# Attention layers with written-out passes, a third bank of scores, and projections moved behind the scores

## The chip, the core and the metric

The kernel runs on one core of a Trainium2 chip. The core has five engines that run side by side: PE (TensorE, matrix products, with PEld for its weight loads), DVE (VectorE), ACT (ScalarE), POOL (GpSimd) and SP (SyncE, which starts DMAs). Each takes its own instructions strictly in order; semaphores make one wait for another. Products land in PSUM, eight banks of 128 partitions x 512 words of 32 bits; only DVE and ACT empty them here. The metric is the device time of one execution in microseconds (us).

## What is computed

Four transformer layers run one after the other on x, 16 sequences of 256 tokens with 128 features. Each adds an attention part and a feed-forward part to x, both fed with the layer-normed x:

```python
xn = _layernorm(x); x = x + attn_0(xn) + ffn_0(xn)   # sparse attention; experts with capacity
xn = _layernorm(x); x = x + attn_1(xn) + ffn_1(xn)   # 16 heads of 64, local mask; 8 experts, top 2
xn = _layernorm(x); x = x + attn_2(xn) + ffn_2(xn)   # 4 heads, windows; gated ternary network
xn = _layernorm(x); x = x + attn_3(xn) + ffn_3(xn)   # 16 heads of 64, causal; linear with a low-rank part
```

The second and the last layer share their attention:

```python
q, k, v = (x @ Wq, x @ Wk, x @ Wv) split into 16 heads of 64
attn = softmax(q @ k.T * 64 ** -0.5 + mask)
out = (attn @ v) joined @ Wo
```

In the second layer each token also passes experts: `relu(x @ up.T) ** 2 @ down.T`, weighted by a gate. In the last layer the linear feed-forward part is folded into the output projection.

## The kernel before

The function `attention` writes both 16-head layers. The work is 8 passes, and a pass has 2 sequences with 8 pairs of heads each, so 16 steps, s = 5 to 20; a `Fori` loop on every engine runs over the passes, and the 16 steps inside it are written out. The stages of one pair are spread over steps, so that step s handles the scores of pair s-2, the transposes of pair s-3 and the values of pair s-4 at once. Before the loop, a straight-line start fills this pipeline.

On PE a step is, in this order: scores of two heads (a mask through the identity matrix L1157, then the products L1160 and L1163 on two row halves of the array, written 64*128 in the trace), values (L1177, L1180, on two column halves, 128*64), six transposes (L1188, full array), in the second layer the experts' up projection (L1198 to L1200), the query and key projection of a later pair (`misc(i, s, "q")`, L1099 to L1101), in the second layer the down projection (L1210), and last what some steps have beside it: turns of the normed x ("t", L1091, s=6 and 14), value projections ("v", L1107 to L1109, s=8 to 11 and 16 to 19), gate logits ("g", L1144, second layer, s=8 and 16) and the output projection ("o", L1114 and L1119, s=12 and 20). Projections whose operands are split into a high and a low part take three matmuls per product.

DVE takes the maxima of the scores (L1358, L1359), copies the transposes out (L1365), inverts the sums (L1370), copies value projections out (L1391) and adds expert and output results to x (L1417, L1427). ACT does the exponentials (L1250, L1251, the sums coming with them), copies a pair's heads out (L1257), applies the experts' relu (L1262), copies queries and keys out (L1269) and turns out (L1236, L1237), in this order within a step. POOL multiplies by the inverted sums (L1472) and squares (L1485).

The order is that of the code; no scheduler changes it. What holds a bank back is a pair of counters per bank, full and empty. In the second layer query/key and value projections share bank 4, so a value projection waits until ACT's L1269 has emptied it. In the last layer values have bank 6. Scores of the two heads of a pair use banks 0 and 1; PE starts the next pair's scores when both heads' exponentials have been taken. Heads come out in bank 5, columns 0 to 255. "t", "g" and "o" use columns 256 to 511 of bank 5 in the second layer (there PE waits besides until the heads have been copied, L1128), and of bank 7 in the last.

Of the kernel before, what the change touches and what calls it, by code (L numbers as in the profile page):

```python
# [69 lines left out]
def program(nc, ins, out, upto=9):  # L70
# [3 lines left out]
    with ctx:  # L74
# [907 lines left out]
        def attention(name, layer, qk, mask, pack, phase, last_layer):  # L982
# [54 lines left out]

            BANK = {"q": 4, "v": 4, "t": 5, "g": 5, "o": 5} if moe else {"q": 4, "v": 6, "t": 7, "o": 7}
            side = PS[BANK["t"]][:, 256:512]
            shared = {}  # L1040
            for bk in sorted(set(BANK.values())):
                items = [m for m in MISC if BANK[m[1]] == bk]
                ahead = (BANK["t"] == bk) + sum(m[0] >= NP for m in items)
                key = {4: "q", 5: "t", 6: "v", 7: "t"}[bk]
                shared[bk] = (heir("at_full_" + key, len(items), ahead), heir("at_empty_" + key, len(items), ahead),
                              {m[1:]: k for k, m in enumerate(items)})
# [37 lines left out]
            def pe_(pe):  # L1084
# [38 lines left out]
                def misc(i, s, kinds):  # L1123
                    for at, kind, n in MISC:
                        if at != s or kind not in kinds:
                            continue
                        if moe and kind in "tgo":
                            pe.wait_ge(s_ot.s, s_ot.at(i, s - 4))  # L1128
# [21 lines left out]
                def step(i, s, least):  # L1150
                    j = s - 2
                    if j >= least:
                        pe.wait_ge(*read(i, "q", j))
                        pe.wait_ge(s_ex.s, s_ex.at(i, 2 * j - 1))
                        q = qp[j % 2]
                        for n in range(2):
                            pe.matmul(PS[n][:, m_from:384], ident16[:, :], mask[:, m_from:384], start=True, stop=False, skip_group_check=True)  # L1157
                        for n in range(2):
                            r = slice(64 * n, 64 * n + 64)
                            pe.matmul(PS[n][:, Q0], q[r, 0:128], q[r, 256:384], start=False, stop=True, skip_group_check=True)  # L1160
                        for n in range(2):
                            r = slice(64 * n, 64 * n + 64)
                            pe.matmul(PS[n][:, Q1], q[r, 128:256], q[r, 256:512], start=False, stop=True,  # L1163
                                      skip_group_check=True).then_inc(s_f.s, 1)
                    j = s - 4
                    if j >= least:
# [5 lines left out]
                        for at_, kind, n in MISC:  # L1172
                            if moe and kind in "tgo" and at_ == (s - 1 if s > FIRST else NP + FIRST - 1):
                                pe.wait_ge(*read(i, kind, n if s > FIRST else n - PER[kind]))
# [16 lines left out]
                    if moe and u >= least:  # L1191
# [9 lines left out]
                        mm.then_inc(f_u.s, 1)  # L1201
                    misc(i, s, "q")
                    u = s - 5
# [19 lines left out]
                pe.sem_inc(full_("o"), 1)  # L1223
                with pe.Fori(0, PASSES) as i:
                    for s in STEPS:
                        step(i, s, 0)

            def act_(act):
# [15 lines left out]
                def step(i, s, least):  # L1244
                    j = s - 2
                    if j >= least:
                        for g in (2 * j, 2 * j + 1):
                            act.wait_ge(s_mx.s, s_mx.at(i, g))
                            act.wait_ge(s_t.s, s_t.at(i, g - 4))
                            act.activation(pr[g % 4][:, Q0], PS[g % 2][:, Q0], ACT.Exp, bias=nmx[:, g % 4, 0:1], accum_out=sm[:, g % 4, 0:1])  # L1250
                            act.activation(pr[g % 4][:, Q1], PS[g % 2][:, Q1], ACT.Exp, bias=nmx[:, g % 4, 1:2],  # L1251
                                           accum_out=sm[:, g % 4, 1:2]).then_inc(s_ex.s, 1)
# [23 lines left out]
                for s in range(NP, NP + FIRST):  # L1276
                    step(-1, s, NP)
                with act.Fori(0, PASSES) as i:
                    for s in STEPS:
                        step(i, s, 0)  # L1280

            def dve_(dve):
# [6 lines left out]
                def settle(i):  # L1289

                    dve.wait_ge(dv.s, dv.before(k[0] - 1) if i is None or isinstance(i, int) else dv.at(i, k[0] - 1))

# [56 lines left out]
                def step(i, s, least):  # L1349
# [4 lines left out]
                    if j >= least:  # L1354
                        for g in (2 * j, 2 * j + 1):
                            dve.wait_ge(s_f.s, s_f.at(i, g))
                            dve.wait_ge(s_ex.s, s_ex.at(i, g - 4))
                            dve.tensor_reduce(nmx[:, g % 4, 0:1], PS[g % 2][:, Q0], AX, ALU.max, negate=True)  # L1358
                            dve.tensor_reduce(nmx[:, g % 4, 1:2], PS[g % 2][:, Q1], AX, ALU.max, negate=True).then_inc(s_mx.s, 1)  # L1359
                    for n in range(2):  # L1360
# [73 lines left out]
                dve.sem_inc(empty_("o"), 1)  # L1434
                with dve.Fori(0, PASSES) as i:
                    k[0] = 0
                    for s in STEPS:
                        step(i, s, 0)
                    assert k[0] == dv.n, (k[0], dv.n)

            def pool_(pool):
# [45 lines left out]
                for s in range(NP, NP + FIRST):  # L1487
                    step(-1, s, NP)
                with pool.Fori(0, PASSES) as i:
                    for s in STEPS:  # L1490
                        step(i, s, 0)
# [549 lines left out]
```

## Time and profile before

| | us |
|---|---|
| median of 3 runs | 2587.78 (2582.88 to 2591.21) |
| the profiled execution | 2596.73 |
| its span, first to last instruction | 2594.9 |
| second layer's steps, about | 694 to 1542 of the span |
| third layer, about | 1542 to 1997 |
| last layer's steps, about | 1997 to 2584 |
| PE busy, share of the span | 2255.4 (87%) |
| DVE, ACT, POOL busy | 1571.1, 1121.9, 1009.6 |
| mean granted clock of TensorE | 0.936 |

A busy time counts an engine's instructions; for PE the ends are modelled and successive matmuls overlap, so the distance from one start to the next tells more than a duration. "Idle before" gives how long an engine stood still ahead of an instruction and which engine's instruction released it; "issue" means that nothing in the profile explains it. The granted clock is 1.00 at 2.4 GHz and 0.50 at 1.2 GHz.

### The profile page before, as it was taken

The page shows a single profiled execution, that of the slowest core. Times are in us where ns is not written, and L with a number is a line of the kernel's source. Part 1 is how long each engine was busy: PE and PEld are TensorE (multiplying, and loading weights), DVE is VectorE, ACT ScalarE, POOL GpSimd, SP SyncE. Part 2 cuts the span into 40 slices and gives each one's busy share as a digit, 9 for nine tenths or more (in the row PEclk, how much of TensorE's full clock was granted, in tenths as well). Part 3 has the DMA queues.
Part 4 walks back from the last instruction along what each step waited for, and adds up shares of the span by engine and source line. Part 5 has one row for each costly group of instructions (what it writes and reads, how often), then busy time and mean ns, then how long its engine had stood idle before and what let it go on. Part 6 is the DMA issues. An engine that isn't in the chain of part 4 may idle for free.

```text
span 2594.9 us, 52767 instructions
## 1 busy us (share of the span) xinstructions
PE 2255.4 (87%) x15426; PEld 1689.0 (65%) x15426; DVE 1571.1 (61%) x4620; ACT 1121.9 (43%) x3580; POOL 1009.6 (39%) x1467
## 2 busy tenths in 40 slices
PE   2688888645599999999999989999997999999998
PEld 2466666423477777777777766666665777777676
DVE  3678877622465556565656556554555676666666
ACT  1233233011344444444544445554554555555554
POOL 2434444056444444444444451111113454444444
PEclk9989898568799999999999999999998999999999
DMA  4100000213300000000000000000000000000001
GB/s 159 35 1 0 0 0 0 71 37 27 108 2 2 2 2 2 1 2 2 2 2 1 2 1 1 0 0 0 0 0 1 2 0 1 1 1 1 1 1 33
DMA packets 31900, 32.56 MB, mean 13 GB/s; under 512 B 5472, under 2 KB 30048, under 8 KB 30816
## 3 DMA queue, kind: packets, MB, share of 16 engines
q1 hardware_dynamic: 26080, 25.99, 3.0%
q0 software_dynamic: 5632, 4.33, 1.3%
q8 instruction: 85, 1.39, 0.2%
q14 instruction: 103, 0.84, 0.1%
HBM read 21.79 MB, written 8.52 MB: 12 GB/s over the span
## 4 chain that ended last, share of the span: by engine, by line
PE 60%; issue 5%; ACT 5%; DVE 5%; POOL 1%; DMA 1%; DVEq 0%; ACTq 0%; SPq 0%; POOLq 0%
PE bank L1188 6%; PE bank L1177 5%; PE bank L1114 4%; PE bank L1163 4%; PE bank L1160 4%; PE bank L1210 4%; PE bank L1157 3%; PE bank L1099 2%; PE bank L1101 2%; PE bank L1100 2%; PE bank L1577 2%; PE bank L1599 2%; PE bank L1180 2%; PE bank L1601 2%; PE bank L1600 2%
## 5 line engine op out<-in xcount | busy, mean ns | idle before, releaser
L1472 POOL TENSOR_TENSOR work<-work 128x128 f32<-128x128 f32 (+1 forms) x1048 | 503.4, 512 | 795.6 <-DVE work L1370 795.6
L1250 ACT ACTIVATE work<-bank,work 128x128 f32<-128x128 f32 x524 | 191.8, 366 | 673.7 <-DVE work L1359 673.7
L1365 DVE COPY work<-bank 128x384 f32<-128x384 f32 x520 | 282.9, 548 | 42.2 <-PE bank L1188 16.3
L1251 ACT ACTIVATE work<-bank,work 128x256 f32<-128x256 f32 x524 | 247.4, 472 | 0.0
L1358 DVE TENSOR_REDUCE work<-bank 128x1 f32<-128x128 f32 x524 | 149.6, 285 | 151.5 <-PE bank L1163 129.2
L1188 PE MATMUL bank<-w_const,work 128*128 128x128 f32 x1560 | 230.8, 285 | 0.0
L1359 DVE TENSOR_REDUCE work<-bank 128x1 f32<-128x256 f32 x524 | 216.6, 413 | 0.0
L1188 PEld LDWEIGHTS bank<-w_const,work 128*128 128x128 f32 x1560 | 168.4, 142 | 46.6 <-issue 46.6
L1391 DVE COPY work<-bank 128x512 f32<-128x512 f32 x136 | 94.0, 691 | 164.4 <-PE bank L1109 155.5
L1177 PE MATMUL bank<-work 128*64 128x256 f32 x1032 | 174.0, 416 | 0.1
L1269 ACT ACTIVATE work<-bank 128x512 f32<-128x512 f32 x266 | 162.3, 610 | 11.8 <-PE bank L1101 10.7
L1099 PE MATMUL bank<-l_xn_hi,l_qk_hi 128*128 128x256 f32 x532 | 164.2, 309 | 2.8 <-DVE l_xn_lo L1314 2.7
L1163 PE MATMUL bank<-work 64*128 64x256 f32 x1048 | 166.2, 395 | 0.0
L1157 PE MATMUL bank<-mask,ident 128*128 128x384 bf16 (+1 forms) x524 | 121.0, 314 | 36.1 <-ACT work L1251 20.7
L1100 PE MATMUL bank<-l_xn_lo,l_qk_hi 128*128 128x256 f32 x532 | 151.6, 285 | 0.0
L1101 PE MATMUL bank<-l_xn_hi,l_qk_lo 128*128 128x256 f32 x532 | 151.1, 284 | 0.0
L1210 PE MATMUL bank<-w_l,work 128*128 128x128 f32 x1024 | 134.9, 275 | 0.0
L1160 PE MATMUL bank<-work 64*128 64x128 f32 x1048 | 134.7, 335 | 0.0
L1485 POOL TENSOR_TENSOR work<-work 128x512 f32<-128x512 f32 x129 | 134.1, 1040 | 0.0
L1160 PEld LDWEIGHTS bank<-work 64*128 64x128 f32 x1048 | 82.7, 193 | 73.5 <-issue 73.5
L1210 PEld LDWEIGHTS bank<-w_l,work 128*128 128x128 f32 x1024 | 125.0, 191 | 0.0
L1417 DVE SCALAR_TENSOR_TENSOR x_sb<-bank,work,x_sb 128x128 f32 x256 | 77.5, 344 | 66.0 <-PE bank L1210 65.6
(330 smaller groups left out, 5414.0 us busy)
## 6 DMA issues: line engine op xcount, KB each, us to landing
w_l<-in_l SPq DMA_DIRECT2D x1, 3210.5 KB, 10.4
w_l<-in_l SPq DMA_DIRECT2D x1, 3080.0 KB, 22.2
w_f<-in_f SPq DMA_DIRECT2D x1, 3072.0 KB, 15.2
x_sb<-in_x SPq DMA_DIRECT2D x4, 512.0 KB, 5.8
normed_rows<-work SPq DMA_DIRECT2D x1, 2048.0 KB, 9.6
residual<-x_sb SPq DMA_DIRECT2D x1, 2048.0 KB, 9.4
qk<-in_qk SPq DMA_DIRECT2D x2, 1024.0 KB, 7.8
x_sb<-residual SPq DMA_DIRECT2D x4, 512.0 KB, 6.0
```

Of the source, the lines that this page charges most:

```text
L1099: pe.matmul(to, qk_hi[:, n, ws], x, start=True, stop=False)
L1100: pe.matmul(to, qk_hi[:, n, ws], xr, start=False, stop=False)
L1101: mm = pe.matmul(to, qk_lo[:, n, ws], x, start=False, stop=True)
L1160: pe.matmul(PS[n][:, Q0], q[r, 0:128], q[r, 256:384], start=False, stop=True, skip_group_check=True)
L1163: pe.matmul(PS[n][:, Q1], q[r, 128:256], q[r, 256:512], start=False, stop=True, skip_group_check=True).then_inc(s_f.s, 1)
L1177: pe.matmul(PS[5][r, 0:256], v[:, 0, h], pt[(2 * j + n) % 4][:, 0:256], start=True, stop=False, skip_group_check=True)
L1188: mm = pe.transpose(PS[2 + g % 2][:, to * 128:(to + 1) * 128], pr[g % 4][:, c * 128:(c + 1) * 128], ident)
L1210: mm = pe.matmul(PS[7][:, t * 128:(t + 1) * 128], h2[u % 2][:, c * 256 + t * 128:c * 256 + (t + 1) * 128], L["down"][:, (2 * e + c) * D:(2 ...
L1251: act.activation(pr[g % 4][:, Q1], PS[g % 2][:, Q1], ACT.Exp, bias=nmx[:, g % 4, 1:2], accum_out=sm[:, g % 4, 1:2]).then_inc(s_ex.s, 1)
L1359: dve.tensor_reduce(nmx[:, g % 4, 1:2], PS[g % 2][:, Q1], AX, ALU.max, negate=True).then_inc(s_mx.s, 1)
L1365: dve.tensor_copy(pt[g % 4], PS[2 + g % 2][:, 0:384]).then_inc(s_te.s, 1)
L1472: ins = pool.tensor_tensor(w, w, spread(rc[:, g % 4, q:q + 1], w.shape[1]), ALU.mult)
```

## The change

Three edits. The four `Fori` loops over the passes become Python loops, so the 8 passes are written out as straight code and every wait compares with a constant. In the last layer three banks (0, 1 and 7) take the scores of heads in turn, and PE's wait for exponentials is one head looser there; the turns and the output projection move from bank 7 to bank 5, with the second layer's waits. In both layers `misc(i, s, "q")` moves from behind the transposes (second layer: from behind the up projection) to right behind the scores. The core of the diff:

```diff
-            BANK = {"q": 4, "v": 4, "t": 5, "g": 5, "o": 5} if moe else {"q": 4, "v": 6, "t": 7, "o": 7}
+            BANK = {"q": 4, "v": 4, "t": 5, "g": 5, "o": 5} if moe else {"q": 4, "v": 6, "t": 5, "o": 5}
+            SCORE = (0, 1) if moe else (0, 1, 7)
+
+            def scored(i, g):
+
+                return PS[SCORE[(i * NH + g) % len(SCORE)]]
...
-                        if moe and kind in "tgo":
+                        if kind in "tgo":
                             pe.wait_ge(s_ot.s, s_ot.at(i, s - 4))
...
-                        pe.wait_ge(s_ex.s, s_ex.at(i, 2 * j - 1))
+                        pe.wait_ge(s_ex.s, s_ex.at(i, 2 * j + 1 - len(SCORE)))
...
-                            pe.matmul(PS[n][:, Q1], q[r, 128:256], q[r, 256:512], start=False, stop=True,
+                            pe.matmul(scored(i, 2 * j + n)[:, Q1], q[r, 128:256], q[r, 256:512], start=False, stop=True,
                                       skip_group_check=True).then_inc(s_f.s, 1)
+                    misc(i, s, "q")
                     j = s - 4
...
-                            if moe and kind in "tgo" and at_ == (s - 1 if s > FIRST else NP + FIRST - 1):
+                            if kind in "tgo" and at_ == (s - 1 if s > FIRST else NP + FIRST - 1):
                                 pe.wait_ge(*read(i, kind, n if s > FIRST else n - PER[kind]))
...
-                    misc(i, s, "q")
                     u = s - 5
...
-                with pe.Fori(0, PASSES) as i:
+                for i in range(PASSES):
                     for s in STEPS:
                         step(i, s, 0)
```

The other engines' uses of `PS[n]` and `PS[g % 2]` for scores become `scored(...)`, and their loops change as PE's does. A line of the kernel before stands 5 lines further down in the changed one up to the scores, and up to 6 further behind them.

Where the instructions stand, in three places. First PE in the second layer, step s=9: from the end of the up projection to the value projection. bank6 holds up, bank4 the projections, bank7 down; the names in brackets are the counters waited for, `at_empty_q` being bank 4's. Before:

```order
L1200 MATMUL bank6<-l1_xn_hi_0_49,l1_up_lo_58 128x256
L1133 REGISTER_ALU
L1099 MATMUL bank4<-l1_xn_hi_1_50,l1_qk_hi_53 128x256 [waits at_normed_split,at_empty_q]
L1100 MATMUL bank4<-l1_xn_lo_1_52,l1_qk_hi_53 128x256
L1101 MATMUL bank4<-l1_xn_hi_1_50,l1_qk_lo_55 128x256
L1099 MATMUL bank4<-l1_xn_hi_1_50,l1_qk_hi_53 128x256
L1100 MATMUL bank4<-l1_xn_lo_1_52,l1_qk_hi_53 128x256
L1101 MATMUL bank4<-l1_xn_hi_1_50,l1_qk_lo_55 128x256
L1210 MATMUL bank7<-w_l1,work 128x128 [waits moe_added,moe_square]
L1210 MATMUL bank7<-w_l1,work 128x128 x3
L1133 REGISTER_ALU
L1107 MATMUL bank4<-l1_wv_hi_54,l1_xn_hi_1_50 128x512 [waits at_normed_split,at_empty_q]
```

and now:

```order
L1205 MATMUL bank6<-l1_xn_lo_0_51,l1_up_hi_57 128x256
L1206 MATMUL bank6<-l1_xn_hi_0_49,l1_up_lo_58 128x256
L1215 MATMUL bank7<-w_l1,work 128x128 [waits moe_added,moe_square]
L1215 MATMUL bank7<-w_l1,work 128x128 x3
L1112 MATMUL bank4<-l1_wv_hi_54,l1_xn_hi_1_50 128x512 [waits at_normed_split,at_empty_q]
L1113 MATMUL bank4<-l1_wv_lo_56,l1_xn_hi_1_50 128x512
L1114 MATMUL bank4<-l1_wv_hi_54,l1_xn_lo_1_52 128x512
```

The six query/key matmuls are gone from between up and down, and the value projection's wait for bank 4 stands where it stood. Second, PE in the last layer, an early step, from the scores on: bank5 takes the values, bank2 the transposes. Before:

```order
L1163 MATMUL bank0<-work 128x256
L1163 MATMUL bank1<-work 128x256
L1167 REGISTER_ALU
L1168 REGISTER_ALU [waits at_turned_out]
L1177 MATMUL bank5<-work 64x256 [waits at_heads_out]
L1177 MATMUL bank5<-work 64x256
L1180 MATMUL bank5<-work 64x128 x2
L1185 REGISTER_ALU
L1186 REGISTER_ALU [waits at_weights]
L1188 MATMUL bank2<-w_const,work 128x128 [waits at_turned_out]
L1188 MATMUL bank2<-w_const,work 128x128 x2
```

and now:

```order
L1168 MATMUL bank7<-work 128x256
L1168 MATMUL bank0<-work 128x256
L1104 MATMUL bank4<-l3_xn_hi_0_67,l3_qk_hi_71 128x256 [waits at_normed_split,at_empty_q]
L1105 MATMUL bank4<-l3_xn_lo_0_69,l3_qk_hi_71 128x256
L1106 MATMUL bank4<-l3_xn_hi_0_67,l3_qk_lo_73 128x256
L1104 MATMUL bank4<-l3_xn_hi_0_67,l3_qk_hi_71 128x256
L1105 MATMUL bank4<-l3_xn_lo_0_69,l3_qk_hi_71 128x256
L1106 MATMUL bank4<-l3_xn_hi_0_67,l3_qk_lo_73 128x256
L1183 MATMUL bank5<-work 64x256 [waits at_heads_out,at_turned_out]
L1183 MATMUL bank5<-work 64x256
L1186 MATMUL bank5<-work 64x128 x2
```

The projections now stand between the row halves of the scores and the column halves of the values, the scores are in banks 7 and 0 here, and the register work of the loop is gone. Third, PE in the last layer at a turn (L1091, which is L1096 in the changed kernel). Before:

```order
L1100 MATMUL bank4<-l3_xn_lo_0_69,l3_qk_hi_71 128x256
L1101 MATMUL bank4<-l3_xn_hi_0_67,l3_qk_lo_73 128x256
L1130 REGISTER_ALU
L1133 ISA [waits at_normed]
L1091 MATMUL bank7<-w_const,work 128x128 [waits at_empty_t]
L1091 MATMUL bank7<-w_const,work 128x128
L1154 REGISTER_ALU [waits at_empty_q]
L1157 MATMUL bank0<-mask3,ident16 128x256 [waits at_exps]
L1157 MATMUL bank1<-mask3,ident16 128x256
```

and now:

```order
L1194 MATMUL bank2<-w_const,work 128x128 [waits at_turned_out,at_weights]
L1194 MATMUL bank2<-w_const,work 128x128 x2
L1194 MATMUL bank3<-w_const,work 128x128 [waits at_turned_out,at_weights]
L1194 MATMUL bank3<-w_const,work 128x128 x2
L1096 MATMUL bank5<-w_const,work 128x128 [waits at_empty_t,at_normed,at_heads_out]
L1096 MATMUL bank5<-w_const,work 128x128
L1162 MATMUL bank1<-mask3,ident16 128x256 [waits at_exps,at_empty_q]
L1162 MATMUL bank7<-mask3,ident16 128x256
```

The turn is in bank 5 with `at_heads_out`, ACT's copy of this step's heads, among its waits, and it follows the transposes directly.

## Rows read from the trace of the kernel before

**Rows 1.** Windows by stage: length, busy us of PE, PEld, DVE, ACT, POOL, clock, DMA

```profile
694.00:1542.00 848.00, 801.18 (x6456) 641.63 (x6452) 507.81 (x1660) 399.93 (x1467) 388.05 (x662) 0.97 0.01 2
...
1997.00:2584.00 587.00, 564.99 (x4652) 423.29 (x4650) 400.14 (x1241) 328.84 (x1322) 270.37 (x550) 0.98 0.00 1
```

**Rows 2.** Waits in the second layer: who waited for whom, us, times, longest

```profile
PE bank L1107 <- ACT work L1269: 33.2, 17, 2.3
...
PE bank L1157 <- issue: 12.8, 7, 2.0
```

**Rows 3.** Waits in the last layer: who waited for whom, us, times, longest

```profile
DVE work L1358 <- issue: 18.9, 7, 2.9
...
PE bank L1157 <- ACT work L1251: 19.4, 16, 2.7
```

**Rows 4.** Timeline, second layer, step s=11: start, us, engine, line, tiles, count [idle]

```profile
948.83 0.28 PE L1200 MATMUL bank<-l_xn_hi,l_up_lo 128*128 128x256 f32 x1
...
948.95 0.28 PE L1099 MATMUL bank<-l_xn_hi,l_qk_hi 128*128 128x256 f32 x1
...
949.34 0.62 ACT L1262 ACTIVATE work<-bank 128x512 f32<-128x512 f32 x1
...
949.66 1.05 PE L1210 MATMUL bank<-w_l,work 128*128 128x128 f32 x8
949.86 0.60 ACT L1269 ACTIVATE work<-bank 128x512 f32<-128x512 f32 x1
...
950.51 0.50 PE L1107 MATMUL bank<-l_wv_hi,l_xn_hi 128*128 128x512 f32 x1
```

**Rows 5.** Timeline of PE, last layer's straight-line start, projections right behind scores

```profile
1988.48 0.60 PE L1163 MATMUL bank<-work 64*128 64x256 f32 x4
1989.01 0.39 PE L1099 MATMUL bank<-l_xn_hi,l_qk_hi 128*128 128x256 f32 x1
...
1989.83 0.40 PE L1107 MATMUL bank<-l_wv_hi,l_xn_hi 128*128 128x512 f32 x1
```

**Rows 6.** Timeline of PE, third layer, from full array to 32-column tiles

```profile
1588.71 0.39 PE L1600 MATMUL bank<-lo_hA,hi_h 128*128 128x512 f32 x1
1588.94 0.39 PE L1601 MATMUL bank<-hi_hA,lo_h 128*128 128x512 f32 x1
1589.26 0.64 PE L1634 MATMUL bank<-work 128*32 128x256 f32 x8
```

**Rows 7.** Timeline, last layer, step s=13: PE, and what ACT does at its end

```profile
2179.67 0.38 PE L1157 MATMUL bank<-mask,ident 128*128 128x256 bf16 x2
...
2180.31 0.60 PE L1163 MATMUL bank<-work 64*128 64x256 f32 x4
...
2180.84 0.65 PE L1177 MATMUL bank<-work 128*64 128x256 f32 x4
...
2182.40 0.36 ACT L1250 ACTIVATE work<-bank,work 128x128 f32<-128x128 f32 x1
...
2183.19 0.39 ACT L1257 ACTIVATE work<-bank 128x256 f32<-128x256 f32 x1
...
2183.37 0.39 PE L1157 MATMUL bank<-mask,ident 128*128 128x256 bf16 x2
```

**Rows 8.** Timeline, second layer, step s=9: the value projection waits

```profile
937.21 0.50 PE L1107 MATMUL bank<-l_wv_hi,l_xn_hi 128*128 128x512 f32 x1 [2.08 <-ACT work L1269]
```

**Rows 9.** Windows, second layer, first 3.69 us of step s=10

```profile
938.01:941.70 3.69, 3.69 (x20) 1.88 (x20) 2.75 (x9) 0.79 (x4) 0.26 (x1) 0.54 0.00 0
```

**Rows 10.** Timeline of PE, last layer, step s=17, which has a value projection

```profile
2194.88 0.39 PE L1157 MATMUL bank<-mask,ident 128*128 128x256 bf16 x2
...
2198.29 0.40 PE L1107 MATMUL bank<-l_wv_hi,l_xn_hi 128*128 128x512 f32 x1
...
2198.98 0.39 PE L1157 MATMUL bank<-mask,ident 128*128 128x256 bf16 x2
```

**Rows 11.** The page: DMA queue, kind, packets, MB, share of the engines

```profile
q8 instruction: 85, 1.39, 0.2%
```

More of the change, by code:

```diff
@@ L1043, in attention @@
                 ahead = (BANK["t"] == bk) + sum(m[0] >= NP for m in items)
-                key = {4: "q", 5: "t", 6: "v", 7: "t"}[bk]
+                key = {4: "q", 5: "t", 6: "v"}[bk]
                 shared[bk] = (heir("at_full_" + key, len(items), ahead), heir("at_empty_" + key, len(items), ahead),
@@ L1153, in step @@
                         pe.wait_ge(*read(i, "q", j))
-                        pe.wait_ge(s_ex.s, s_ex.at(i, 2 * j - 1))
+                        pe.wait_ge(s_ex.s, s_ex.at(i, 2 * j + 1 - len(SCORE)))
                         q = qp[j % 2]
                         for n in range(2):
-                            pe.matmul(PS[n][:, m_from:384], ident16[:, :], mask[:, m_from:384], start=True, stop=False, skip_group_check=True)
+                            pe.matmul(scored(i, 2 * j + n)[:, m_from:384], ident16[:, :], mask[:, m_from:384], start=True, stop=False, skip_group_check=True)
                         for n in range(2):
                             r = slice(64 * n, 64 * n + 64)
-                            pe.matmul(PS[n][:, Q0], q[r, 0:128], q[r, 256:384], start=False, stop=True, skip_group_check=True)
+                            pe.matmul(scored(i, 2 * j + n)[:, Q0], q[r, 0:128], q[r, 256:384], start=False, stop=True, skip_group_check=True)
                         for n in range(2):
                             r = slice(64 * n, 64 * n + 64)
-                            pe.matmul(PS[n][:, Q1], q[r, 128:256], q[r, 256:512], start=False, stop=True,
+                            pe.matmul(scored(i, 2 * j + n)[:, Q1], q[r, 128:256], q[r, 256:512], start=False, stop=True,
                                       skip_group_check=True).then_inc(s_f.s, 1)
+                    misc(i, s, "q")
                     j = s - 4
@@ L1249, in step @@
                             act.wait_ge(s_t.s, s_t.at(i, g - 4))
-                            act.activation(pr[g % 4][:, Q0], PS[g % 2][:, Q0], ACT.Exp, bias=nmx[:, g % 4, 0:1], accum_out=sm[:, g % 4, 0:1])
-                            act.activation(pr[g % 4][:, Q1], PS[g % 2][:, Q1], ACT.Exp, bias=nmx[:, g % 4, 1:2],
+                            act.activation(pr[g % 4][:, Q0], scored(i, g)[:, Q0], ACT.Exp, bias=nmx[:, g % 4, 0:1], accum_out=sm[:, g % 4, 0:1])
+                            act.activation(pr[g % 4][:, Q1], scored(i, g)[:, Q1], ACT.Exp, bias=nmx[:, g % 4, 1:2],
                                            accum_out=sm[:, g % 4, 1:2]).then_inc(s_ex.s, 1)
@@ L1277, in act_ @@
                     step(-1, s, NP)
-                with act.Fori(0, PASSES) as i:
+                for i in range(PASSES):
                     for s in STEPS:
@@ L1289, in settle @@
                 def settle(i):
-                    dve.wait_ge(dv.s, dv.before(k[0] - 1) if i is None or isinstance(i, int) else dv.at(i, k[0] - 1))
+                    dve.wait_ge(dv.s, dv.before(k[0] - 1) if i is None or i < 0 else dv.at(i, k[0] - 1))
                 def stats(i, tile):
@@ L1357, in step @@
                             dve.wait_ge(s_ex.s, s_ex.at(i, g - 4))
-                            dve.tensor_reduce(nmx[:, g % 4, 0:1], PS[g % 2][:, Q0], AX, ALU.max, negate=True)
-                            dve.tensor_reduce(nmx[:, g % 4, 1:2], PS[g % 2][:, Q1], AX, ALU.max, negate=True).then_inc(s_mx.s, 1)
+                            dve.tensor_reduce(nmx[:, g % 4, 0:1], scored(i, g)[:, Q0], AX, ALU.max, negate=True)
+                            dve.tensor_reduce(nmx[:, g % 4, 1:2], scored(i, g)[:, Q1], AX, ALU.max, negate=True).then_inc(s_mx.s, 1)
                     for n in range(2):
@@ L1434, in dve_ @@
                 dve.sem_inc(empty_("o"), 1)
-                with dve.Fori(0, PASSES) as i:
+                for i in range(PASSES):
                     k[0] = 0
@@ L1488, in pool_ @@
                     step(-1, s, NP)
-                with pool.Fori(0, PASSES) as i:
+                for i in range(PASSES):
                     for s in STEPS:
```

## The prediction

> **What bounds the kernel now.** I read the windows by stage first. In the second layer PE is busy 801 of 848 us, in the last layer 565 of 587 us, while DVE, ACT and POOL stay at or under 69% of either stage [rows 1]. So these two stages run at PE's pace, and a change there is worth what it does to the stretch from one step's first L1157 to the next. The waits say what is left over. In the second layer PE sat idle 33.2 us in 17 waits before the value projection L1107, for ACT's copy L1269 out of bank 4, and 12.8 us in 7 waits before a scores group L1157 with nothing named ("issue"): seven is the number of times that an eight-pass loop jumps back [rows 2]. In the last layer DVE sat 18.9 us before L1358 on "issue", again 7 times, and PE then waited 19.4 us for the exponentials [rows 3]: there the loop's end is paid by DVE and handed on.
>
> **Term 1: the written-out loops.** They remove 14 loop ends, 7 in each layer (the eighth leaves the loop). The idle time that the view shows is 12.8 and 19.4 us. A matmul row of 0.28 us hides the next start by about 0.17 us, since those of one kind start 0.12 us apart [rows 4], so an idle interval is longer than shown by that: 7 times 0.17 makes 14 us in the second layer, 16 times 0.17 makes 22 us in the last. Gain 36 us. It could be less if DVE's and PE's new straight code ran into late instruction loads, at most all 36.
>
> **Term 2: the projections behind the scores.** No instruction is added, but a change of how PE's array is divided is. A step now goes: mask on the full array, scores on two row halves (64*128), values on two column halves (128*64), transposes, projections on the full array, which is three switches. After the change it goes full, rows, full, columns, full: four. The straight-line start of the last layer already holds the new sequence's first half: from L1163 to L1099 0.53 us, and from there to the next full matmul 0.82 us [rows 5]. In its old place the same six matmuls take 0.71 us (948.95 to 949.66) [rows 4]. The switch from full to columns stands in the third layer: L1601 is followed after 0.32 us by L1634, where two full ones stand 0.23 us apart, so 0.09 us [rows 6]. From L1163 to L1177 is 0.53 us today [rows 7]. New: 0.53 + 0.82 + 0.09 = 1.44 us; old: 0.53 + 0.71 = 1.24 us. So 0.20 us more in each step that PE bounds. L1634 has 32 columns and not 64, so the last 0.09 is by a neighbour; its bounds are 0 and the 0.11 that the row switch adds (0.82 less 0.71), and a step costs between 0.11 and 0.22 us. I take 0.20.
> The Trainium skill's page "TensorEngine Tiling (Array Packing)", under Key Properties, says that changing the tiling mode drains TensorE. It gives no price; by it the switch can't be free, and it speaks against this edit where PE is the bound. The rows above agree, with 0.09 to 0.11 us.
>
> **Term 3: in the second layer ACT's copy comes later.** ACT takes a step's work in a fixed order: exponentials, heads, relu L1262 of the up projection, then L1269, which empties bank 4. The value projection needs that bank and ends PE's step. In step s=11 all fits: relu at 949.34, L1269 from 949.86 to 950.46, L1107 at 950.51 without a wait [rows 4]. After the change the up projection stands behind the moved one. Its last L1200 starts at 948.83 + 0.71 + 0.20 = 949.74 and ends 0.28 us later, 950.02; relu at about 950.06, L1269 0.52 us after it at 950.58, over at 951.18, L1107 at 951.23. PE is there at 950.51 + 0.20 = 950.71. That is a wait of 0.52 us where there was none. It meets value steps s=8, 10, 11, 16, 18 and 19. In s=9 and 17 PE already waits 2.08 us, for an ACT that the gate work on DVE made late [rows 8]; up is long done there, so L1107 keeps its time and the 0.20 of term 2 disappears in the wait.
> Per pass: 8 steps without values at 0.20 = 1.6 us, six at 0.72 = 4.3 us, two at 0: 5.9 us, times 8 = 47 us. Less 14 from term 1: the second layer loses 33 us. The waits of 2 us are followed by a stretch of 3.69 us at a granted clock of 0.54, one level being 1.2 and the other 2.4 GHz [rows 9]; since these waits shrink by 0.2 us only, I leave both stretches of a pass in place.
>
> **Term 4: three banks of scores in the last layer.** A value step is bound by PE: 3.41 us up to L1107 and 4.10 us in all [rows 10]. A step without values takes 3.70 us, so it waits 0.29 us for the exponentials of the step before [rows 7]. With a third bank it need only wait for the first head of the pair. ACT is through with that one about when it starts the second (2182.40), and with both about when it turns to L1257 (2183.19) [rows 7]: 0.8 us earlier, so the wait goes. But the step then costs 3.41 + 0.20 = 3.61 us. Four such steps (s=5, 7, 13, 15) gain 0.09 each, 0.4 us; eight value steps lose 0.20 each, 1.6 us.
>
> **Term 5: what the third bank pushes out.** The turns (s=6, 14) and the output projection (s=12, 20) move from bank 7 to the second half of bank 5, and PE must first wait until ACT has copied this step's heads out (L1257). In s=13 that copy starts 3.52 us after the step's first L1157 and takes 0.39 us [rows 7]: the bank is free at 3.96, PE would be there at 3.61. A turn step today is 3.70 us too, its two turns hidden in the exponentials' wait; it becomes 3.96 + 0.22 = 4.18, so 0.48 more. An output step pays 0.20 + 0.35 = 0.55 more. Together 2.1 us a pass. If ACT is as late as it may be, 0.3 us more on each of the four; if early, 0.35 less: between 0.7 and 3.3 us. The reader's side (the next values wait for DVE's or ACT's reading) is covered by scores and projections, 1.44 us.
> Last layer per pass: -0.4 + 1.6 + 2.1 = 3.3 us, times 8 = 26 us, less 22 from term 1: 4 us slower.
>
> **Covers.** POOL's products start after DVE's copies of the transposes, which come 0.9 us later in a step; the next step's transposes are later by the same, so nothing is late. The scores wait for nothing new. The last layer's mean granted clock is 0.98 [rows 1], so at most 2% of 587 us, 12 us, are lost to half clock; without the waits of 2 us at its loop ends these stretches should go, but part of them lies in waits already counted in term 1. I take a third, -4 us (0 to -12).
>
> **The sum.** 33 + 4 - 4 = +33 us on the profiled execution, whose span is 2594.9 us and its time 2596.73. The median of the runs is 2587.78, 9 us lower; I let the difference carry over: 2621 us.
>
> **Rivals.**
> A, the switches are free (PE drains while it would wait anyway). The term of 0.20 goes everywhere, the waits of terms 3 and 5 stay: second layer 6 x 0.52 x 8 = 25, less 14; last layer (-0.29 x 4 + 2 x 0.48 + 2 x 0.55) x 8 = 7, less 22. With -4 for the clock: 11 - 15 - 4 = -8 us, 2580 us. Rows 5 and 6 speak against it.
> B, faster: neither switch nor wait costs, because straight code with constant waits lets ACT and PE run ahead. Then the loop ends (36) and the exponentials' waits (0.29 x 6 x 8 = 14) are gained, and 4 of the clock: 2534 us; with term 5 left in, 2551 us. For it speaks that the loop ends are real; against it that inside a step PE's starts are as close as in the straight-line start: L1163 to its follower is 0.53 us in both [rows 5, 7], so registers cost nothing there. It decides once a moved projection costs under 0.1 us a step and ACT's relu is not held up.
> C, the clock: the new waits of 0.5 us bring more half-clock stretches. Two more in each pass of the second layer cost 3.69 x 0.46 = 1.7 us each, 27 us: 2648 us. The other way, the two that are there could go: 2594 us.
> D, instruction loads. The straight code of both layers must be streamed. The page has 85 loads of 16 KB for one queue already [rows 11], as loops ask for their code in every pass, and the stretches of rows 4, 7 and 10 show no gap that a load would make; so I give a loss little. 
>
> **Chances.** Forecast 0.50 with its own range 2605 to 2640; A 0.13; B 0.12; C slower 0.10, C the other way 0.07; D 0.08. A change of 0.3% is 8 us. Faster by more than that: B and half of A, 0.18; within: the other half of A and a part of C's second way, 0.10; slower: the rest, 0.72. The range that leaves out most of B and the far end of C and D is 2568 to 2648.
>
> **What would show it.** In a profile of the changed kernel: no "issue" waits before the scores (term 1); scores to values 1.44 us with the projection between (2); a wait of about half a microsecond before the value projection in 6 more steps of each pass, ended by ACT's copy (3); no exponentials' wait in the last layer, steps of 3.6 and 4.3 us (4); the turns and the output projection waiting for the copy of the heads (5). The prediction is wrong if the second layer does not grow, or if a step without values there stays at its present length.

## The result: 1.1% slower

The changed kernel takes 2614.91 us (median of 4 runs, 2611.14 to 2617.06), the kernel before 2586.33 us (4 runs, 2582.88 to 2591.21). The ratio is 1.0108 with a 95% interval of 1.0087 to 1.0128, so it is 28.6 us slower; forecast were 2621 us and +33. In all that follows a ratio is to the kernel before on the same chip; 0.01 of it is 26 us. Lines behind the second layer's bank table stand 5 or 6 higher than before: L1157 is now L1162, L1163 L1168, L1099 L1104, L1177 L1183, L1107 L1112, L1200 L1206, L1262 L1267, L1269 L1274, and the copy of the heads L1257 is L1262.

The page of the profiled execution after (span; busy time of each engine; the first queue that loads instructions):

```profile
span 2615.3 us, 48911 instructions
...
PE 2298.1 (88%) x15410; PEld 1700.0 (65%) x15426; DVE 1521.8 (58%) x4620; ACT 1134.9 (43%) x3580; POOL 1012.5 (39%) x1467
...
q8 instruction: 103, 1.69, 0.3%
```

The span is 2615.3 us against 2594.9, and the loads of [rows 11] went from 85 to 103. A second queue that loads instructions went the other way, from 103 to 91, at half the bytes per load.

Windows over the eight passes of the second and of the last layer, from the first step's scores to the end of the last step; columns as in [rows 1]. First the kernel before, with its edges at these same points, then the kernel after:

```profile
696.20:1540.60 844.40, 798.44 (x6434) 639.24 (x6432) 504.73 (x1649) 397.74 (x1458) 386.54 (x660) 0.97 0.01 2
1999.20:2584.90 585.70, 563.68 (x4641) 422.35 (x4640) 398.29 (x1235) 327.02 (x1314) 269.75 (x549) 0.98 0.00 1
```

```profile
692.00:1556.30 864.30, 823.61 (x6434) 646.25 (x6432) 483.47 (x1651) 408.20 (x1458) 388.56 (x661) 0.98 0.01 1
...
2012.80:2605.50 592.70, 581.36 (x4642) 424.66 (x4639) 371.40 (x1237) 329.54 (x1317) 271.56 (x549) 1.00 0.01 2
```

The second layer grew from 844.4 to 864.3 us, +19.9, and the last from 585.7 to 592.7, +7.0. Together that is more than the difference of the spans (20.4): by the same edges, what lies ahead of the second layer came out 4.2 us shorter and the third layer 2.1. In the nine profiled executions of this document the second layer's first step of a pass (s=5) starts between 688.4 and 703.4 us, though the code ahead of it is the same, so 4.2 us there say nothing. PE's busy time rose by 25 us and 18 us, although the matmuls are the same (x6434; x4641 and x4642): most of the time that the moved projections cost in PE's order shows here as PE at work, not as a wait (how long a matmul lasts is modelled).

The waits after, in the second layer (who waited for whom: us in all, times, longest):

```profile
PE bank L1112 <- ACT work L1274: 40.7, 64, 1.7
```

Before, L1269 held L1107 for 33.2 us in 17 waits [rows 2]. Now the copy holds the value projection in 64 places, 8 in each pass, for 40.7 us. The row "issue" before the scores is gone in both layers, and so is PE's wait for the exponentials in the last [rows 2, 3]. What stands in the last layer instead:

```profile
PEld bank L1119 <- ACT work L1262: 7.4, 16, 0.5
PEld bank L1096 <- ACT work L1262: 6.9, 15, 0.5
...
PE bank L1104 <- DVE l_xn_lo L1319: 3.9, 15, 0.3
```

The first two are the output projection and the turns waiting for the copy of the heads. The third, for DVE's low part of the normed rows, was in no term.

Timeline after, second layer, s=11, which answers to [rows 4]:

```profile
943.41 0.50 PE L1162 MATMUL bank<-mask,ident 128*128 128x384 bf16 x2
...
944.17 0.60 PE L1168 MATMUL bank<-work 64*128 64x256 f32 x4
...
944.70 0.39 PE L1104 MATMUL bank<-l_xn_hi,l_qk_hi 128*128 128x256 f32 x1
...
945.61 0.65 PE L1183 MATMUL bank<-work 128*64 128x256 f32 x4
...
947.73 0.28 PE L1206 MATMUL bank<-l_xn_hi,l_up_lo 128*128 128x256 f32 x1
...
948.04 0.60 ACT L1267 ACTIVATE work<-bank 128x512 f32<-128x512 f32 x1 [0.59 <-PE bank L1206]
...
948.54 0.59 ACT L1274 ACTIVATE work<-bank 128x512 f32<-128x512 f32 x1
...
949.18 0.50 PE L1112 MATMUL bank<-l_wv_hi,l_xn_hi 128*128 128x512 f32 x1 [0.28 <-ACT work L1274]
...
949.99 0.50 PE L1162 MATMUL bank<-mask,ident 128*128 128x384 bf16 x2
```

From the scores L1168 to the values L1183 it is 945.61 - 944.17 = 1.44 us, with the projection L1104 between. The up projection's last L1206 starts at 947.73; behind it relu L1267, then the copy L1274 from 948.54 to 949.13, then L1112. The step is 6.58 us long (949.99 - 943.41), where the kernel before has 5.89: 0.69 more. Less the 0.20 that scores to values took, PE lost 0.49 us ahead of L1112. The trace calls only 0.28 us of it idle, since the matmul before hides the rest (as in term 1).

Timeline after, last layer, s=13, which answers to [rows 7]:

```profile
2198.10 0.38 PE L1162 MATMUL bank<-mask,ident 128*128 128x256 bf16 x2
...
2201.63 0.39 ACT L1262 ACTIVATE work<-bank 128x256 f32<-128x256 f32 x1
2201.69 0.27 PE L1162 MATMUL bank<-mask,ident 128*128 128x256 bf16 x1
```

The next scores start 3.59 us after the step's first ones, before the copy of the heads (2201.63) is done; before it was 3.70 us and, as the prediction reads [rows 7], they waited for the exponentials.

### The profile page after: what moved, and what is told of

Read it like the earlier page. It is cut to its first block, busy times and chain, and to the rows that moved or that the text cites. A ratio compares the mean times of both kernels' runs of the same rounds, so it can differ in the third digit from the quotient of the medians.

```text
span 2615.3 us, 48911 instructions
## 1 busy us (share of the span) xinstructions
PE 2298.1 (88%) x15410; PEld 1700.0 (65%) x15426; DVE 1521.8 (58%) x4620; ACT 1134.9 (43%) x3580; POOL 1012.5 (39%) x1467
## 3 DMA queue, kind: packets, MB, share of 16 engines
q8 instruction: 103, 1.69, 0.3%
## 4 chain that ended last, share of the span: by engine, by line
PE 64%; DVE 13%; issue 10%; ACT 7%; POOL 3%; DMA 2%; DVEq 1%; SPq 0%; POOLq 0%; ACTq 0%
PE bank L1194 6%; PE bank L1183 5%; PE bank L1119 5%; PE bank L1168 4%; PE bank L1104 4%; PE bank L1165 4%; PE bank L1162 2%; PE bank L1215 2%; PE bank L670 2%; PE bank L1106 2%; PE bank L1105 2%; PE bank L1112 2%; PE bank L1604 2%; PE bank L1186 2%; PE bank L1582 2%
## 5 line engine op out<-in xcount | busy, mean ns | idle before, releaser
L1256 ACT ACTIVATE work<-bank,work 128x256 f32<-128x256 f32 x524 | 247.2, 472 | 0.0
L1104 PE MATMUL bank<-l_xn_hi,l_qk_hi 128*128 128x256 f32 x532 | 181.0, 340 | 7.1 <-DVE l_xn_lo L1319 6.8
L1183 PE MATMUL bank<-work 128*64 128x256 f32 x1032 | 172.6, 414 | 0.0
L1104 PEld LDWEIGHTS bank<-l_xn_hi,l_qk_hi 128*128 128x128 f32 x532 | 103.0, 194 | 99.4 <-issue 64.2
L1274 ACT ACTIVATE work<-bank 128x512 f32<-128x512 f32 x266 | 161.5, 607 | 5.8 <-PE bank L1106 5.8
L1168 PE MATMUL bank<-work 64*128 64x256 f32 x1048 | 161.8, 386 | 0.0
L1162 PE MATMUL bank<-mask,ident 128*128 128x384 bf16 (+1 forms) x524 | 115.9, 303 | 0.2 <-ACT work L1256 0.2
## 6 DMA issues: line engine op xcount, KB each, us to landing
w_l<-in_l SPq DMA_DIRECT2D x1, 3210.5 KB, 10.4
w_l<-in_l SPq DMA_DIRECT2D x1, 3080.0 KB, 22.1
```

Source lines behind the costliest of these rows:

```text
L1104: pe.matmul(to, qk_hi[:, n, ws], x, start=True, stop=False)
L1168: pe.matmul(scored(i, 2 * j + n)[:, Q1], q[r, 128:256], q[r, 256:512], start=False, stop=True, skip_group_check=True).then_inc(s_f.s, 1)
L1183: pe.matmul(PS[5][r, 0:256], v[:, 0, h], pt[(2 * j + n) % 4][:, 0:256], start=True, stop=False, skip_group_check=True)
L1256: act.activation(pr[g % 4][:, Q1], scored(i, g)[:, Q1], ACT.Exp, bias=nmx[:, g % 4, 1:2], accum_out=sm[:, g % 4, 1:2]).then_inc(s_ex.s, 1)
```

## The experiments

Each is told by its edit to the changed kernel. Medians of 5 or 6 runs; the kernel before had 11 on each of the two chips, with medians of 2593.11 us (the first four) and 2591.01 us (the last three). The expectations were written in us for a kernel before at about 2586 us, so it is the ratio that is to be compared. Lengths of steps and of passes come from one profiled execution of each kernel. They run from the first mask matmul (L1157, now L1162) of one step to that of the next, and where no timeline stands beside it, a length given for a step is the median of the 8 passes.

**1. The written-out loops alone.** The banks, the waits and the place of the projections are as before:

```diff
-"t": 5, "o": 5}
-SCORE = (0, 1) if moe else (0, 1, 7)
+"t": 7, "o": 7}
+SCORE = (0, 1)
...
-misc(i, s, "q")      # behind the scores
...
+misc(i, s, "q")      # behind the up projection
```

> Alone the written-out passes: two banks of scores, turns and output projection in bank 7, projections where they stood. If term 1 of the prediction is right, the second layer loses its 7 loop ends (14 us) and the last its 7 with the half-clock stretches behind them (22 + 4 us): 2586 - 40 = 2546 us, with step lengths as before (5.11 and 3.70 us). Rival, instruction loads: straight code stalls for its loads, steps are longer here and there and the time stays above 2570 us.

Measured: 2551.14 us, 0.9834 [0.9819, 0.9849], 43 us faster by the ratio. That is the whole of term 1 with the clock, and rival D is out: the loads are the 103 and 91 of the changed kernel, and PE, DVE, ACT and POOL show no wait on "issue" over 0.3 us in the two layers. Timeline of PE, last layer, s=13 again:

```profile
2151.93 0.38 PE L1162 MATMUL bank<-mask,ident 128*128 128x256 bf16 x2
...
2155.72 0.38 PE L1162 MATMUL bank<-mask,ident 128*128 128x256 bf16 x2 [0.24 <-ACT work L1256]
```

The step is 3.79 us, and the wait of 0.24 for the exponentials is there. The kernel before has 3.70 [rows 7], so written out these steps (s=13 to 15) are 0.08 us longer and not as before; why, no run tells. The median step s=20 of the second layer went from 10.75 to 8.70 us, and s=5 of the last from 5.96 to 3.79: a loop end cost 2.1 to 2.2 us. The remainder is the clock, and waits of s=9 and 17 that became 0.1 to 0.2 us shorter. Waits in the second layer, and windows behind two of them, s=9 in two passes (columns as in [rows 9]):

```profile
PE bank L1112 <- ACT work L1274: 31.7, 24, 1.9
```

```profile
931.60:935.20 3.60, 3.60 (x32) 2.63 (x32) 3.36 (x12) 1.10 (x6) 0.27 (x1) 1.00 0.00 0
982.25:985.85 3.60, 3.60 (x20) 1.60 (x18) 2.17 (x8) 0.00 (x0) 0.26 (x1) 0.61 0.02 5
```

The value projection waits 1.88 us ahead of the first window and 1.87 ahead of the second. Behind one wait the granted clock is 1.00, 2.4 GHz; behind the other 0.61 over 3.6 us, most of it at 1.2 GHz. Of the 24 waits, 16 are those of s=9 and 17. 8 of these 16 have the low clock behind them; before it was 15 of 16, where the wait was 2.00 to 2.29 us. The other 8 waits are in s=10 and 18, where these are at the full clock. The kernel before shows this wait once, since all but one of these steps have a half-clock stretch in them. Timeline of PE in kernel 1, s=10 of the second pass:

```profile
829.15 0.50 PE L1162 MATMUL bank<-mask,ident 128*128 128x384 bf16 x2
...
834.65 0.50 PE L1112 MATMUL bank<-l_wv_hi,l_xn_hi 128*128 128x512 f32 x1 [0.21 <-ACT work L1274]
...
835.46 0.50 PE L1162 MATMUL bank<-mask,ident 128*128 128x384 bf16 x2
```

This step is 6.31 us long, and s=18 the same where it is at the full clock; s=11, with the same work on PE and no wait, is 5.89.

**2. The changed kernel without the move.**

```diff
-misc(i, s, "q")      # behind the scores
...
+misc(i, s, "q")      # behind the up projection
```

> The changed kernel with the projections back at their old place (written-out passes and three banks stay). Theory, the moved projections cost 0.20 us a step by one more switch of the array's division and half a microsecond more in value steps: a second-layer step without values is 5.11 us again, its value steps 5.89 us, a last-layer value step 4.10 us, and the time is 2586 - 14 (second layer) - 26 + 7 (last layer: turns 0.48 and output projections 0.55 us longer, four steps a pass 0.29 shorter) = 2553 us. Rival, the move is free and the written-out code is what costs: the time stays near 2615 us.

Measured: 2553.66 us, 0.9837 [0.9820, 0.9854]. Against 1.0108 the move costs 0.027, 70 us; by the steps of the two traces it is 45.5 us in the second layer and 23.6 in the last. A pass of the second layer is 102.4 us here (the median) and 106.1 to 109.2 with the move, one of the last layer 71.1 and 74.1. Against kernel 1 this one has the third bank and the wait for the heads, and nothing comes of them: 0.9837 and 0.9834. The timeline of PE in s=13 tells why:

```profile
2151.43 0.38 PE L1162 MATMUL bank<-mask,ident 128*128 128x256 bf16 x2
...
2154.84 0.39 PE L1162 MATMUL bank<-mask,ident 128*128 128x256 bf16 x2
```

3.41 us instead of 3.79, as the third bank promised, four times a pass; but the turn steps went from 3.78 to 4.26 us and the output steps from 7.47 to 8.10.

**3. The changed kernel with two banks** (the bank table and the waits of before, the move stays).

```diff
-"t": 5, "o": 5}
-SCORE = (0, 1) if moe else (0, 1, 7)
+"t": 7, "o": 7}
+SCORE = (0, 1)
```

> The changed kernel with two banks of scores and with turns and output projection back in bank 7. Theory, the third bank gains 0.1 us in four steps of a last-layer pass and pays 0.4 to 0.65 us in each of four others for bank 5: without it a pass is about 72.2 us and not 74.1, so 15 us less, 2600 us; the second layer stays as it is after the change. Rival, the third bank pays by taking the wait for exponentials away: the last layer is longer than 593 us and the time above 2615 us.

Measured: 2608.98 us, 1.0054 [1.0038, 1.0069]. With the move in place the third bank and its wait lose 0.0054, 14 us. A pass of the last layer is 72.6 us against 74.1: with two banks a turn step is 3.80 us (4.25), an output step 7.62 (8.11), and steps without values 3.79 (3.59).

**4. ACT's copy ahead of the relu.** In the changed kernel ACT empties bank 4 first and then takes the up projection:

```diff
+for part in ("q", "tg"):
     u = s - 4
-    if moe and u >= least:
+    if part == "tg" and moe and u >= least:
         act.wait_ge(f_u.s, f_u.at(i, u))
 ...
         act.activation(h1[u % 2], PS[6][:, :], ACT.Relu)
+    emptied(i, s, part)      # "q": the copy out of bank 4
```

> The changed kernel with one order turned round on ACT in the second layer: the copy that empties bank 4 stands ahead of the experts' relu. Theory, the value projections of s=8, 10, 11, 16, 18 and 19 wait half a microsecond because that copy stands behind a relu that waits for the late up projection: these waits go (6 x 0.52 x 8 = 25 us) and those of s=9 and 17 shrink by 0.5 us (8 us): 2615 - 33 = 2582 us; if the half-clock stretches behind s=9 and 17 go too, 20 us less, 2562 us. Rival, the value steps are longer for another reason (the switch, DVE's copy): they stay at 6.58 us and the time at 2615 us.

Measured: 2576.90 us, 0.9926 [0.9911, 0.9941]: 0.018 or 47 us of the loss gone. Timeline, second layer, s=11:

```profile
938.41 0.50 PE L1162 MATMUL bank<-mask,ident 128*128 128x384 bf16 x2
...
942.32 0.62 ACT L1256 ACTIVATE work<-bank 128x512 f32<-128x512 f32 x1
...
943.03 0.60 ACT L1282 ACTIVATE work<-bank 128x512 f32<-128x512 f32 x1
...
943.64 0.48 PE L1112 MATMUL bank<-l_wv_hi,l_xn_hi 128*128 128x512 f32 x1
...
944.43 0.50 PE L1162 MATMUL bank<-mask,ident 128*128 128x384 bf16 x2
```

In this kernel L1256 is the copy and L1282 the relu. The copy starts at 942.32, the relu at 943.03, and L1112 at 943.64 with no wait. The step is 6.02 us, 0.56 less than after. The waits of the layer:

```profile
PE bank L1112 <- ACT work L1256: 22.9, 16, 1.4
```

Only the 16 of s=9 and 17 are left, the longest 1.4 us. Six steps at 0.55 and two at 0.26 a pass make 31 us; the other 15 are the clock, since behind a wait of 1.43 us not one of the 16 stretches is at 1.2 GHz, where the changed kernel has 10. Expected were 0.52 us in the six steps and 0.5 in the two.

**5. The projections behind the transposes.** One line lower than in the changed kernel, behind the values and transposes but ahead of the up projection. There no switch is added, while ACT's copy is as late as after the change:

```diff
     misc(i, s, "q")      # behind the scores: taken out
 ...
                 mm.then_inc(s_t.s, 1)
+    misc(i, s, "q")
     u = s - 4
```

> The changed kernel with the projections not behind the scores but right behind the transposes (in the second layer still ahead of the up projection; in the last layer that is their old place). This takes away the fourth switch of the array's division and keeps the late up projection. Theory: steps without values are 5.11 us again, the value steps s=8, 10, 11, 16, 18, 19 keep about 0.5 us of wait for ACT's copy (6.4 us in s=11), which is 6 x 0.52 x 8 = 25 us over the kernel with the projections at their old place: if that one is 0.984 of the kernel before, this one is 0.994. Rival, the whole cost is the switch: 0.984. Other rival, the switch costs nothing and the place among full-array work does not matter: 5.31 us steps and 1.011.

Measured: 2569.37 us, 0.9922 [0.9899, 0.9946]. Timeline, second layer, s=11:

```profile
940.83 0.50 PE L1162 MATMUL bank<-mask,ident 128*128 128x384 bf16 x2
...
941.58 0.60 PE L1168 MATMUL bank<-work 64*128 64x256 f32 x4
...
942.11 0.65 PE L1182 MATMUL bank<-work 128*64 128x256 f32 x4
...
945.75 0.59 ACT L1274 ACTIVATE work<-bank 128x512 f32<-128x512 f32 x1
...
946.39 0.50 PE L1112 MATMUL bank<-l_wv_hi,l_xn_hi 128*128 128x512 f32 x1 [0.28 <-ACT work L1274]
...
947.20 0.50 PE L1162 MATMUL bank<-mask,ident 128*128 128x384 bf16 x2
```

Scores and values are 0.53 us apart, the step is 6.37 us: 0.21 less than after, and 0.48 more than before. So the two costs of the move are apart: 0.20 us for the place between scores and values, which is where the added switch is, and 0.48 for the late copy. In the last layer, where nothing waits for that copy, the steps are those of kernel 2.

**6. The gate work later.** Kernel 1, in which DVE does its gate work (which made ACT late in s=9 and 17) four steps later, in s=12 and 20, when PE is at its longest step:

```diff
-if at != s or kind not in "vg":
+if kind not in "vg" or s != at + (4 if kind == "g" else 0):
 ...
-dve.wait_ge(g_w.s, g_w.at(i, u // E1 - 2))
+dve.wait_ge(g_w.s, g_w.at(i, u // E1))
 ...
-act.wait_ge(g_w.s, g_w.at(i, n - 2))
+act.wait_ge(g_w.s, g_w.at(i, n - 1))
```

> Written-out passes alone, and DVE does the gate work of the second layer four steps later, in s=12 and s=20, beside the output projection. Theory: the long steps s=9 and 17 and the half-clock stretches behind them come from DVE's gate work ahead of the maxima. Without it these steps and s=10 and 18 are 5.89 us like s=11, a pass is 96.3 us and not 102.4, 49 us less than with written-out passes alone: 0.965 of the kernel before. Rival, the wait is ACT's own backlog: s=9 stays near 8 us, 0.983.

Measured: 2507.82 us, 0.9688 [0.9665, 0.9712]. Timeline, second layer, s=9:

```profile
910.28 0.48 PE L1162 MATMUL bank<-mask,ident 128*128 128x384 bf16 x2
...
914.70 0.60 ACT L1274 ACTIVATE work<-bank 128x512 f32<-128x512 f32 x1
...
915.35 0.50 PE L1112 MATMUL bank<-l_wv_hi,l_xn_hi 128*128 128x512 f32 x1
...
916.16 0.34 PE L1162 MATMUL bank<-mask,ident 128*128 128x384 bf16 x1
```

The value projection starts 0.65 us behind the copy's start, with no wait; the step is 5.88 us and was 8.16. In kernel 1 it was 7.96. Against that kernel the ratio is 38 us better, and 49 were expected, for two reasons. Steps s=10 and 18 are 6.32 us and not 5.89: the wait of 0.22 ahead of their value projection stayed, so DVE's gate work is not its cause. (In s=10 of this kernel DVE takes the layer norm's statistics, L1300, from 917.48 us on and the maxima only behind them, from 917.99; that this makes ACT late was not tested.) And the first pass is 4.2 us longer than the others, since PE now waits 2.65 us for DVE in its s=5:

```profile
693.92 0.65 PE L1182 MATMUL bank<-work 128*64 128x256 f32 x4 [2.65 <-DVEq L1439]
```

Behind that wait stands the one half-clock stretch that the layer's passes still have. Kernel 7 has the same wait (2.64 us) and no such stretch.

**7. The third bank without the wait.** Kernel 6 with three banks of scores in the last layer, but the turns and the output projection in bank 6, which holds the values' projection, in place of the second half of bank 5:

```diff
-"v": 6, "t": 7, "o": 7}
-SCORE = (0, 1)
+"v": 6, "t": 6, "o": 6}
+SCORE = (0, 1) if moe else (0, 1, 7)
```

> As the run with the later gate work, and in the last layer three banks of scores with turns and output projection in bank 6 beside the value projections, without the wait for the copy of the heads; query and key projections at their old place. Theory: with no wait for bank 5 the third bank pays: steps without values 3.41 us and not 3.79, turns 3.63, output projections 7.46, a pass of 68.6 us and not 70.5, 15 us less: 0.959 of the kernel before. Rival, sharing bank 6 brings new waits of the same size: 0.965 or more.

Measured: 2493.51 us, 0.9627 [0.9604, 0.9651]: 97 us faster than the kernel before, the best of all. Against kernel 6 it is 0.006, or 16 us by the ratio and 15 by the steps of the last layer, as expected; 0.959 was missed by what kernel 6 had missed already. Windows over the second and the last layer:

```profile
703.40:1483.20 779.80, 773.71 (x6434) 628.80 (x6432) 521.80 (x1659) 396.19 (x1458) 386.50 (x660) 1.00 0.01 2
...
1941.40:2490.20 548.80, 548.80 (x4642) 418.25 (x4640) 398.93 (x1235) 326.77 (x1314) 269.93 (x549) 1.00 0.01 2
```

779.8 and 548.8 us, against 844.4 and 585.7 before, PE busy 99 and 100%. Timeline of PE, last layer, s=13 and the turn step s=14:

```profile
2112.88 0.38 PE L1162 MATMUL bank<-mask,ident 128*128 128x256 bf16 x2
...
2116.27 0.39 PE L1162 MATMUL bank<-mask,ident 128*128 128x256 bf16 x2
...
2119.68 0.38 PE L1096 MATMUL bank<-w_const,work 128*128 128x128 f32 x2
...
2119.89 0.27 PE L1162 MATMUL bank<-mask,ident 128*128 128x256 bf16 x1
```

3.39 and 3.62 us: the turns' matmul L1096 stands right ahead of the next scores and waits for nothing.

## Why the prediction was right, and where by other sums

**Term 1, the loops: right in sum, by other parts.** Forecast were -36 us, and -4 for the clock; kernel 1 gives -43. In its trace the second layer is 24.7 us shorter, where 14 were forecast, and the last 22.1, where 22 + 4 were (from the first step's scores to those of the last step). In the second layer s=20 gives 13.9 us, as forecast; the other 10.8 stand in s=9, 10, 17 and 18. There the waits fell (2.08 to 1.88 us in s=9) and 7 stretches less went at half clock, 8 in place of 15. I had left that layer's stretches in place.

**Term 2, the switch: right to 0.01 us.** 1.44 us from scores to values was the forecast and is what s=11 shows. A step without values in the second layer went from 5.11 to 5.31 us, one with values in the last from 4.10 to 4.30. Kernel 5, which moves the same six matmuls without adding a switch, takes the 0.20 away. It shows that the place between scores and values costs the 0.20. That this is the switch, and nothing else about the place, is read from [rows 5] and [rows 6]; no run puts the matmuls at another boundary. What the Trainium skill's page "TensorEngine Tiling (Array Packing)" says under Key Properties, that changing the tiling mode drains TensorE, agrees with this.

**Term 3, the late copy: right in place and nearly in size; the layer's sum was not.** 0.52 us was forecast for six steps a pass; s=11 shows 6.58 - 5.89 - 0.20 = 0.49, kernel 5 0.48 and kernel 4 0.55. Against kernel 1 the whole move costs this layer 44.5 us, forecast 47. But the layer came out at +19.9 us against the kernel before and not at +33, and 12 of the 13 us are in four steps of each pass.

I had forecast 0.72 us for s=9 and 10 together, and the same for s=17 and 18, 11.5 us in all; measured, the 16 pairs together became 0.5 us shorter. At the full clock such a pair is 14.56 us in the kernel before (the one case that it has), 14.27 in kernel 1 and 14.54 after: the written-out loops had taken off what the move then put on, and s=10 and 18 had a wait already (0.21 us shown in kernel 1), so the move lengthened them by only 0.27 us at the full clock (6.31 to 6.58), in place of 0.72. The clock adds little to the difference: 10 half-clock stretches in place of 15, but each costs 1.5 us and not 1.0 to 1.1. So the step of the prediction that was off is this: that s=10 and 18 have no wait before the change, as s=11 has none, and its last sentence, "since these waits shrink by 0.2 us only, I leave both stretches of a pass in place". The wait shown in s=9 went from 2.08 to 1.69 us, and 6 of 16 stretches were at the full clock, which is rival C's other way in number but not in its price.

**Terms 4 and 5, the third bank: right, with one wait missing.** Steps without values: 3.59 us, forecast 3.61. Turn steps: +0.54, forecast +0.48. Output steps: +0.65, forecast +0.55. What I missed is s=8 and 16, 4.59 us where the other value steps are 4.30. Timeline there:

```profile
2173.13 0.60 PE L1168 MATMUL bank<-work 64*128 64x256 f32 x4
...
2173.44 0.40 DVE L1319 TENSOR_TENSOR l_xn_lo<-work,l_xn_hi 128x256 fp32r<-128x256 f32 x1
...
2173.99 0.36 PE L1104 MATMUL bank<-l_xn_hi,l_qk_hi 128*128 128x256 f32 x1 [0.26 <-DVE l_xn_lo L1319]
```

The first projections of the next sequences' rows need what DVE's L1319 makes. In their old place they came behind the transposes and never met it; moved up, L1104 waits. 16 times 0.3 are 5 us, which with the turns and outputs makes the last layer +7.0 in place of 0 (4, less 4 for the clock). I had written "the scores wait for nothing new" and asked the same of the projections nowhere.

**The rivals.** A, free switches, fell by the 1.44 us and by kernel 5. B, that straight code lets all run ahead, fell by the 64 waits of L1112. D fell by kernel 1: 18 more loads than before and no wait beside them. That the errors are of opposite sign, -13 us in the second layer and +7 in the last, helps the sum, and so does luck. The forecast of +33 us was made for profiled executions, and those are 20.4 us apart in span. The medians are 28.6 apart, because the profiled execution before was 10.4 us over its median and the one after only 2.2, where I had carried the whole difference over. The other stages were 6.5 us shorter in the profiled execution; where the second layer starts differs by 15 us between executions of all these kernels, so it is no gain to count on.

## What to carry to other kernels

Where PE sets the pace, count the changes of its array's division in one step before moving a group of matmuls: one more went with 0.20 us in each of some 200 steps here, and it shows in no wait. Then follow what the moved group fills: the copy that empties its bank stands in another engine's fixed order, and moving the matmuls without the copy turned their head start into 0.5 us of waiting. The spare bank paid only where what it pushed out found a home that no one was late to empty: bank 6 in kernel 7, not bank 5.

## What the runs showed of the hardware

The half clock followed the longer waits of PE, but the wait alone does not decide it. Behind the wait before the value projection in s=9 and 17 the granted clock fell to 1.2 GHz in 15 of 16 cases where the trace showed 2.00 to 2.29 us of idle (before), in 8 and 7 of 16 at 1.88 us (kernels 1 and 2), in 5 of 16 in kernel 5 with the same 1.88, in 10 of 16 at 1.69 (after) and in 13 of 16 at 1.69 in kernel 3, whose code for this layer is the same. At 1.43 us it fell in none (kernel 4), and at 2.64 and 2.65 us, once each, not in kernel 7 but in kernel 6. Within one execution, too, passes whose steps agree to 0.01 us differ in it. So neither the length of the wait nor the work of the steps around it settles the matter, and what does stays open; a count of one profiled execution is no property of a kernel. One such stretch costs 1.5 us in the changed kernel (a pair s=9 and 10 of 16.07 us and not 14.54) and 1.1 in kernel 1 (15.4 and 14.27), where it covers the 0.21 us of wait shown in s=10.

Writing eight passes out in straight code on four engines took the instructions executed from 52767 to 48911 and the loads of 16 KB from 85 to 103; a second queue's loads, of half that size, went from 103 to 91. In the passes of the two layers PE, DVE, ACT and POOL showed no wait on "issue" over 0.3 us after the change.
